# Group 0's attention and second expert pass moved up behind its own feed-forward, in a three-lane kernel whose engine orders are written out

## The reference

```
x = x + 0.5 * fp4_ffn(layernorm(x))        # gate, up, down, inner width 352, blockwise FP4 rounding of activations and weights
x = x + mamba(layernorm(x))                # 2 layers: rmsnorm, in projection, causal conv, selective scan (16 states, 256 channels), out projection
x = x + 0.5 * fp4_ffn(layernorm(x))
x = x + 0.5 * experts(layernorm(x))        # 8 experts, 128 -> 512 -> 128, weight = sigmoid gate where it is over 0.5
x = x + attention(layernorm(x))            # 16 heads of 8 channels, relative bias, causal
x = x + 0.5 * experts(layernorm(x))
```

## Time and profile before

| what | value |
|---|---|
| time, median of 3 runs | 2610.5 us (2609.67 to 2610.94) |
| the profiled execution | 2610.92 us, its span 2609.1 us |
| TensorE busy | 2392.5 us (92%) |
| VectorE busy | 1866.3 us (72%) |
| ScalarE busy | 1559.5 us (60%) |
| GpSimd busy | 1368.1 us (52%) |
| warm-up matmuls (L1351) | 3632, 445.3 us of TensorE's busy time |
| mamba layers end, of groups 0 to 7 (second layers) | 281.7, 525.8, 803.4, 1087.5, 1377.9, 1662.6, 1944.0, 2205.8 us |
| attention added, groups 0 to 7 (L1030) | 805.7, 1085.3, 1380.2, 1664.9, 1946.3, 2189.3, 2393.5, 2528.3 us |

### The profile page before, as it was taken

One profiled execution on the slowest core, in us unless ns is written; L12 is line 12 of the kernel. 1 busy time (PEld: TensorE's weight loads), 2 busy tenths in 40 slices (PEclk: granted clock), 3 DMA queues, 4 the chain that ended last, 5 costly groups with the idle time before them and its releaser, 6 DMA issues.

```text
span 2609.1 us, 40448 instructions
## 1 busy us (share of the span) xinstructions
PE 2392.5 (92%) x14313; PEld 1680.7 (64%) x14313; DVE 1866.3 (72%) x3817; ACT 1559.5 (60%) x3377; POOL 1368.1 (52%) x1227
## 2 busy tenths in 40 slices
PE   7999997997898999889898989999898999988988
PEld 7878884685565666656565656666575656666675
DVE  5879797789587978698687968797879777322220
ACT  1424435543686558664886668665876685566654
POOL 1466483947373856558373847476564737212001
PEclk9999998998899999999899999999999999989999
DMA  4123131312220222112230222121311422100100
GB/s 152 56 76 108 48 97 37 101 46 85 79 90 31 82 86 93 37 63 76 90 90 30 89 86 86 41 79 65 105 54 58 126 60 71 34 20 1 49 5 5
DMA packets 97640, 175.30 MB, mean 67 GB/s; under 512 B 11957, under 2 KB 23133, under 8 KB 95646
## 3 DMA queue, kind: packets, MB, share of 16 engines
q1 hardware_dynamic: 97438, 172.71, 21.6%
HBM read 157.44 MB, written 15.23 MB: 66 GB/s over the span
## 4 chain that ended last, share of the span: by engine, by line
PE 66%; DVE 12%; ACT 11%; POOL 6%; issue 5%; DMA 0%; SPq 0%; POOLq 0%; DVEq 0%; ACTq 0%
PE c_bank L912 15%; PE c_bank L920 14%; PE c_bank L1351 8%; PE a_bank L758 7%; PE a_bank L748 3%; PE b_bank L1060 3%; DVE hst L706 2%; POOL prod_c L829 2%; PE a_bank L727 2%; PE b_bank L580 2%; PE b_bank L1050 1%; ACT weighted_y L955 1%; POOL prod_c L834 1%; PE b_bank L1099 1%; PE b_bank L561 1%
## 5 line engine op out<-in xcount | busy, mean ns | idle before, releaser
L829 POOL TENSOR_TENSOR prod_c<-hst,prod_c 128x512 f32<-128x512 f32 x512 | 670.9, 1318 | 382.0 <-DVE hst L706 362.4
L706 DVE TENSOR_TENSOR_SCAN hst<-dA,a_bank 128x512 f32<-128x512 f32 x512 | 621.1, 1213 | 9.6
L920 PEld LDWEIGHTS c_bank<-w,hid 128*128 128x128 f32 x4096 | 506.8, 196 | 75.7 <-ACT hid L947 38.6
L912 PE MATMUL c_bank<-c_xT,w 128*128 128x512 f32 x1024 | 534.4, 628 | 21.7 <-ACT hid L947 12.1
L920 PE MATMUL c_bank<-w,hid 128*128 128x128 f32 x4096 | 523.0, 280 | 7.6 <-ACT hid L947 7.5
L818 ACT ACTIVATE dA<-delta,a_neg 128x510 f32<-128x510 f32 x512 | 365.2, 719 | 269.1 <-DVE hst L706 260.4
L1351 PEld LDWEIGHTS c_bank<-ident 128*128 128x128 f32 x3632 | 439.1, 194 | 36.1 <-issue 27.2
L1351 PE MATMUL c_bank<-ident 128*128 128x128 f32 x3632 | 445.3, 277 | 1.7 <-ACT weighted_y L955 1.7
L947 ACT ACTIVATE hid<-c_bank,b 128x512 f32<-128x512 f32 x512 | 349.6, 687 | 150.8 <-PE c_bank L912 148.8
L971 POOL TENSOR_TENSOR xs<-xs,weighted_y 128x512 f32<-128x512 f32 x128 | 166.2, 1298 | 426.3 <-ACT weighted_y L955 424.7
L700 DVE TENSOR_TENSOR a_bank<-du,a_bank 128x512 f32<-128x512 f32 x512 | 348.5, 681 | 37.1 <-PE a_bank L748 35.6
(11 more groups left out here) (177 smaller groups left out, 2814.5 us busy)
## 6 DMA issues: line engine op xcount, KB each, us to landing
prod_c<-c_rows SPq DMA_DIRECT2D x512, 256.0 KB, 3.2
q_and_k<-qk_rows SPq DMA_DIRECT2D x64, 192.0 KB
qk_rows<-att_buf SPq DMA_DIRECT2D x40, 256.0 KB, 2.6
w<-in_w SPq DMA_DIRECT2D x2, 2048.0 KB
xs<-in_x SPq DMA_DIRECT2D x8, 256.0 KB, 6.7
bias<-skew SPq DMA_DIRECT2D x1, 2048.0 KB, 8.0
qk_rows<-b_xn SPq DMA_DIRECT2D x8, 256.0 KB, 3.0
out_dram<-xs SPq DMA_DIRECT2D x8, 256.0 KB, 2.4
```

Source lines behind the costliest of these rows:

```text
L706: nc.vector.tensor_tensor_scan(hst[:, s % RS, :], dA[:, s % RA, :], b_bank, 0.0, ALU.mult, ALU.add).then_inc(M.h.sem, 1)
L829: nc.gpsimd.tensor_tensor(prod[:, s % RP, :], hst[:, s % RS, :], cring[:, s % RC, :], ALU.mult).then_inc(M.pp.sem, 1)
L912: nc.tensor.matmul(S.bank[up_bank(e, c)][:, :], w1[:, e, c * 128:(c + 1) * 128], S.xT[:, :], start=True, stop=True).then_inc(M.up.sem, 1)
L920: ins = nc.tensor.matmul(S.bank[down_bank(f)][:, t * D:(t + 1) * D], hid[:, f % 2, j, t * 128:(t + 1) * 128], w2[:, f, j, :], start=(j == ...
```

## The change

In `b_order` and `moe_order`, group 0's attention (2, 0) now stands directly behind (1, 0) and (0, 2), and its second expert pass (1, 0) directly behind the first. All other attentions and second expert passes stay one group late, as before. The lists read

```diff
 ORDER_PE = (
-    "b2d8bd38bd4b2d6b2d6b2d28bd4b3d39b6d57adba3b2d9b2ad5ab2a2d9ad16bd12ab2d3bdad7ad28a2d3ad8adad4ad12a2d8ad14a2"
...
+    "b2d9bd45bd4b2d6b2d6b2d29bd4b3d39b5dbd57adbdaba2bd4b2d3ad6b2ad4a2d10ad13bd13adb2d3bd2ad7ad30a2d11ad15a2d7ad3"
...
 ORDER_SP = (
-    "a165b2ab2a64cacb4a61caca4b4a65c2ab4a65cab4a50b2a2b2a14ca33b4cb4c2")
+    "a132b4a66c2a33b4a64cacab4a65c2ab4a60ca6b4a50baba3b2a12ca33b4cb4c2")
...
-        moe_order = [(0, 0)]
-        b_order = [(0, 0), (0, 1), (1, 0), (0, 2)]
-        for g in range(1, GROUPS):
-            moe_order += [(0, g), (1, g - 1)]
-            b_order += [(1, g), (0, g + 2), (2, g - 1)]
+        prompt = 1
+        moe_order, b_order = [], [(0, 0), (0, 1)]
+        for g in range(GROUPS):
+            moe_order.append((0, g))
+            b_order += [(1, g), (0, g + 2)]
+            if g < prompt:
+                b_order.append((2, g))
+                moe_order.append((1, g))
+            elif g > prompt:
+                b_order.append((2, g - 1))
+                moe_order.append((1, g - 1))
         moe_order.append((1, GROUPS - 1))
         b_order = [o for o in b_order if o[1] < GROUPS] + [(2, GROUPS - 1)]
```

More of the change, by code:

```diff
@@ new lines @@
+    "acabcb2acbacacbcab2cbac2bcab2acba2c2bcab2cbacabcb2acba2c2bac2b2a2bad6bd3b2a2bababd2bd2bd2babd7abd4bd37caca3b"
+    "cb2c2ab2c2ab2a2c2ac2bcb3a2cac5a2c4ac3ab5aba2c2ac2ac2ac2a2c2ac3ba2b3aca2c4aca2c2ac2a2cac3a2c2ac2a2cacbc2b2c3a"
+    "b2a2cbacbcacb2acba2bd3b2a2bad5bd3b3ac2bab2cbc2bab2cbc2bcacb2aba2bc2b2cbc2acbcab2cba2bcb2acbc2bc2b2abcabcac2"
+    "b2a2bc2ac2a2cac2acbcab2a2bcabcab2cbacacac2acacabcbacabacbacabacbac3a2cbca2bac2ac2a2cac2a2c2aca2c2a3d18ad22a"
+    "c2ac12bc2b2c2b2c2b2c7bcb3c11b5cbc12bc2b3c15bcb4cbc2bc2b2cbc2bc2b2cbc2bcb2cbc2bc2b2cbc2bcb2cbc2bc2b2cbc2bc2b2"
@@ new lines @@
+ORDER_POOL = (
+    "ab5a2b2a7ba92bab2a18ba7ba7ba3ca11ba2baca4ca7ca9ca6ca6ca6ca3ca3ba3baba50bacab3a3ba4ca4ba3ca3ca8ca2ba2ca5ca3ba"
+    "ca3ca3ca6babcbaca3caba5baca7cba8ca4cacbaca11ba5bab2c2a4ca9ca6ca9ca9ca3ca10bcab2a4caba3ca2ba6ca3baca6ca5caba3"
+    "ca3ca3ca3ba4bab2c2a5ca8ca8ca9ca8ca5ca7bcab2a4caba3ca2ba4ca5baca7ca3caba6ca3c2a2ba5bab2aca3ca7ca7ca8ca9ca7ca4"
+    "ca5bcab2aca2cabaca5ba4ca4cba8ca4cabaca3ca8ba5bab2c2a7ca9ca9ca5ca7ca4ca9bcab2a3ca2ba3ca2ba4ba3ba3ca2ca4ca4ca8"
+    "ca3ca3ca5caca6ca9ca10ca6ca9ca3ca3ca2b2cbc2bcb3c13bcb2c17")
```

126 lines of the change are left out of this document (59 added, 67 removed).

## The result

The changed kernel takes 2602.4 us (median of 13 runs, 2598.5 to 2607.9) against 2610.75 (13 runs, 2609.1 to 2613.9): ratio 0.9969, 95% interval 0.9961 to 0.9977, so 8.3 us or 0.3% faster. I forecast 2615, slower. The interval also shows that a change of 0.1% can be told here; my text had put that limit at 0.2%. The profiled execution took 2602.0 us, its span is 2600.2 against 2609.1. Lines of the kernel after are those of before plus 8 (L715 is L723, L758 is L766, L764 is L772, L1351 is L1359, L829 and L834 are L837 and L842).

A forecast was written before the change was run, and what follows sets the result against it. No single engine bounds it: sixteen serial mamba layers, each stretched by interleaved work, plus a tail. Terms 9 + 2 - 4.5 - 4 + 0 + 2 + 7 - 7 = +4.5 on 2610.9 give 2615.4, 2615 against the median; range 2597 to 2633.

The forecast's parts named there:

- Group 1's second layer: Attention 0's head now stands ahead of the projection and split at this layer's end: +9 us, least +4, most +14.
- Group 7's second layer: 40 warm-ups, ten attention steps, table loads and a projection behind the expert pass's head: +10 us, from +3 to +16.
- the tail: Last stretch, after the mamba layers: expert pass (1, 5)'s transpose starts some 6 us earlier, -7 us, bounds 0 and -15.
- group 4's first layer: It gets very nearly the sequence group 3's first layer has in the kernel before, with six more warm-ups: -7.5 us.
- the rival of the hidden projection: Group 1's +9 is given back because attention's head would otherwise stand in group 2: 2606 us, chance 0.12.
- Group 3: First layer, with fewer warm-ups and no end of attention 0, 143 for 148.7 us; second +1.2; together -4.5.
- Group 2: +2: First layer, with attention 0's steps, 138.5 against 139.3 us; second, with expert pass and both feed-forwards, 141 against 138.3.
- the early start pays: Group 2 comes out at its lower bounds, 130 and 135 us, 14.5 less than taken: 2601 us, chance 0.12.
- group 4's second layer: Six expert steps and 17 warm-ups more, a pair of table loads fewer: +3.5 us.
- group 6: Order strings the same or nearly, with ten more warm-ups: +2 us.
- The warm-ups lengthen it: Only half the added 43 us of TensorE warm-ups fall into idle time, the rest is +21: 2632 us, chance 0.19.
- The rival of the clock: Filled gaps recover a third of the clock loss in seven second layers, 16 us: 2599 us, chance 0.12.

The follow-up runs named there:

- e3: Kernel after, with projection and add ahead of the attention or expert head at group 1's and group 7's ends, 9 warm-up steps for 22: 2610.0 us, ratio 1.0008.
- e7: Kernel after, group 1's end turned as in e3, with warm-ups and next layer's input product refitted: 2604.9 us, ratio 0.9976.
- e10: As e7, with group 2's x and dt products also ahead of attention 0's first scores: 2602.4 us, ratio 0.9973.
- e4: Kernel after without the 297 warm-up steps of group 2's first layer: 2608.0 us, ratio 1.0002 to the kernel before.
- e1: Kernel after up to the end of group 3's second layer, then the kernel before's step orders: 2614.0 us, ratio 1.0020.
- e5: Kernel after up to the end of group 4's second layer, then the kernel before's step orders: 2604.1 us, ratio 0.9972.
- e6: Kernel before up to the end of group 4's second layer, then the kernel after's step orders: 2613.4 us, ratio 1.0008.
- e13: Kernel after, group 4's first layer with attention 2's first rstd ahead of GpSimd's last two products, its statistics step earlier on VectorE: 2616.6 us, ratio 1.0020.
- e14: Kernel before, group 4's first layer with the mamba's last steps brought forward on TensorE, VectorE, GpSimd and ScalarE queues: 2614.1 us, ratio 1.0011.
- e11: Kernel after without 100 warm-up steps ahead of the last state sums of group 1's and group 7's second layers: 2605.6 us, ratio 0.9983.

## Why the prediction was wrong

**Right.** Group 1's second layer (+8.4 for +9), step by step to within 1.2 us (the largest miss is the last expert add, which ends at 513.3 and not at 512.1). Group 7's second layer (+11.3 for +10) and the tail (-8.5 for -7). In size alone, group 4's first layer (-7.8 for -7.5), on which more below. In e3, e7 and e10 the projection of group 1 was brought forward and the time came back in the next layer; and in the kernel after itself group 1's +8.4 stands. So the rival of the hidden projection is out as it was written.

**Right by luck.** Group 3, -4.3 for -4.5: I had -5.7 in the first layer and +1.2 in the second, and they came out at -2.1 and -2.2. In the first layer my sum for VectorE, 144 to 147, was the right one, and I took 143, below it, for the sake of the warm-ups that leave; TensorE then stood idle for 23.0 us of that layer (146.60 less 123.65), not 10 to 15. Why the second became shorter, no run shows.

**The step that failed: "Group 2: +2".** It was -5.0. Its first layer was taken at 138.5, "against 139.3", from 81 steps at 0.29 and 21 at 0.45 (109 us of VectorE) and 29.5 of standstill. Measured: 103.9 busy and 25.4 of standstill, 129.3. The steps were 5.1 too dear, the standstill 4.1 too large; e4 shows that without the warm-ups, at a clock of 0.78, the standstill is 133.9 - 103.2 = 30.7, about what I had taken. My upper bound, 36.1, came from a layer in which attention shares TensorE with experts at a clock of 0.95. Against that layer the standstill is 5.4 less without experts, even at 0.78, and another 5.3 less with the warm-ups. The attention was done at 651.3, the layer 12.5 us behind it. The second layer was 2.3 above my 141, and varies by 3.3 with the same strings. The rival "the early start pays" named this layer's lower bound, 130; its second layer it put at 135, and that was wrong. Even so the move as a whole gave only -0.6 by the end of group 3.

**The second: "+3.5" for group 4's second layer and "+2" for group 6.** Group 4's second layer was +0.4; there I added up expert steps and warm-ups that lie beside other work, and did not see the new order of its scans and first scores, worth about 8 us from the first scores on (101.3 for 109.5). Groups 5 and 6 together were -3.8 for +2. Of that 3.3 is the clock in group 5's first layer, which can come or not (above); group 6, which has the ten more warm-up steps, became 3.5 shorter, and group 5's second layer 3.0 longer, which I had at 0. With these and the step before put right, the sum of my terms would have been 4.5 - 7.0 - 3.1 - 5.8 = -11.4, and group 7 (+4.4, of it 3.1 in the first layer, +0.1 for my -3), the tail (-1.5) and smaller ones (+0.3 at the start, -0.6 and +0.2 in groups 1 and 3, -0.3 in group 4's first layer) bring it to the measured -8.9.

**The sign.** Up to group 3 I forecast +6.5 and -0.6 came; behind it -2 and -8.3 came. By e1, e5 and e6 the gain is made in group 4's strings. I had the size of its first layer right and the reason only by likeness ("gets very nearly the sequence that group 3's has"). The mechanism is shown by e13 for GpSimd's queue: 9.5 us, the fall of the clock that comes with it included. What VectorE's and TensorE's order does is not shown by itself: e14, with all queues turned, won 4.2 us in the layer, and my version of it paid in the next. What the kernel after has and e14 has not is the second layer's order, with its scans begun 12.7 us earlier beside the same first scores; by these times it makes up for an attention head that starts later in relation to the layer. That part is read from the traces and not tested by itself.

**Warm-ups and clock.** "The warm-ups lengthen it" is refuted: the time fell with 181 steps more, and removing 100 of them (e11) wins nothing (about 3 us slower, within the intervals). Removing 297 (e4) costs 0.33% by the two ratios, some 8 us; between the two profiles it is 6.3, of which 4.6 stands in group 2's first layer and 1.9 in its second, where the same strings vary by as much. The rival of the clock was right in kind: 0.957 to 0.968. The Trainium skill's page "TensorE: Matmul & The Clock Gate", section "What's actually happening", says that activity releases the throttle; by this rule the runs agree, with 2.05 against 3.35 us for the same 16 matmuls. How much of the 8.3 us the clock is, stays open: 4.6 in group 2's first layer and 3.3 in group 5's can be pointed to, and they are part of the stretches counted above, not an addition to them.

## What to carry to other kernels

When orders written out for several in-order queues are planned anew, cost the places that come out differently, not only the move that gave the occasion: here strings two groups behind the move held the gain, and at one layer end a small step put ahead of two others on GpSimd, busy for 53% of the time, was worth 9.5 us. A serial step can be brought forward on every queue and still gain nothing if a second chain, here attention from its first scores on, ends the stretch; look for the chain's own start before costing its neighbour. Warm-ups are counted for a schedule: who moves the work behind them must count them again, or they hold it up or let the clock fall.
